# One scattered array for a routed layer's expert outputs, added up in memory, instead of eight arrays added up on VectorE

## The chip, the cores and the metric

The kernel runs on one core of a Trainium2 chip. A core has five engines with a queue of instructions each: TensorE (PE), VectorE (DVE), ScalarE (ACT), GpSimd (POOL) and SyncE (SP). They meet only at semaphores. SP and POOL also issue DMAs, which 16 DMA engines carry out. The metric is the device time of one execution in microseconds (us), as the median of the runs shown. "PEclk" in a view of the profile is the granted TensorE clock as a share of 2.4 GHz.

## The reference

Two layers run one after the other on a batch of 8 x 256 tokens of 128 numbers (float32). Each layer adds an attention-like block and a routed feed-forward block to its input. The change lies in the first layer:

```
xn  = layernorm(x)
x   = x + _L0_attn_ref(xn, ...)          # a selective scan over 256 positions, 16 states, 256 channels
        + _L0_ffn_ref(xn, ...)           # 8 experts
...
# _L0_ffn_ref
scores = softmax(xt @ Wr)                # [2048 tokens, 8 experts]
G, idx = top_k(scores.T, 512)            # every expert takes its 512 best tokens
X_in   = xt[idx]
h      = gelu(einsum('ekd,edh->ekh', X_in, W1) + b1)
X_e    = einsum('ekh,ehd->ekd', h, W2) + b2
out    = zeros.at[idx.reshape(-1)].add(G[..., None] * X_e)
```

Within one expert a token occurs at most once; several experts may take the same token, so their rows for it have to be added.

## The kernel before

The first layer goes through three stages. In the first (up to some 88 us) the tokens are normalized, the scan's inputs are made and the 512 tokens of each expert are found. The second is the **expert stage** (88 to 185 us), the third the **scan**, in 8 batches of 16 steps (185 to 375 us). The second layer follows.

**The expert stage.** For each expert e (0 to 7):

- DVE compares numbers for a one-hot table (`one_hot`, L541), PE turns it into a list of tokens (`compact`, L1216), DVE writes the list (`indices`, L548 and L549).
- POOL issues four indirect DMAs (`gather(e, q)`, L1976), 128 token rows each, from the array `token_rows` in HBM into `xg[e]`. There are four buffers `xg`, so gather e waits for expert e - 4 (`ye_ready`).
- PE turns the rows over (`turn_rows`, L1225), multiplies (`up0`, L1234), ACT applies the gelu (L1755), PE multiplies again (`down0`, L1243; it signals `d_ready`).
- DVE adds the bias and multiplies by the gate (`gated(e)`, L559 and L561) into one of two buffers `ye[e % 2]`, and signals `ye_ready`. From expert 2 on it first waits until the rows that were put from this buffer before have landed (`added0` or `added1`).
- POOL issues four indirect DMAs (`put(e)`, L2013) that write the 512 rows of `ye` to their tokens' places in an array of that expert, `expert_rows{e}`, in HBM. SP has filled the eight arrays with zeros in the first stage (L936, 1 MB each).
- SP reads the whole array back (`rows_in(e)`, 1 MB, L966 and L969) into staging space, and DVE adds it to the sum `acc` in four instructions (`row_sum(e)`, L565). Experts 0 to 5 are added between the `gated` of later experts, the last ones before the scan's first instruction; expert 6 in batch 1 and expert 7 in batch 2, behind steps 3, 5, 7 and 9.

The order in each queue is written out by hand. POOL's is: gathers 0 to 3, put 0, gather 4, put 1, gather 5, and so on to gather 7, put 4, put 5, put 6, a small product (`pro_c`, L1967), put 7, and then the scan. `AHEAD` is 3. DVE's is: `indices(e + 3)`, `gated(e)`, `one_hot(e + 4)`, `row_sum(e - 2)`; ahead of `gated(7)` it makes four bands for the first batch (`band`, L533).

**The scan.** In each step DVE runs two scan instructions on the step's ring slot (L615), POOL multiplies the slot by the C rows (L1988), PE adds it up (`y_pair`, L1185), and ACT fills the slot for the next batch (L1700). PE makes the scan's other input (`fill`, L1175) two steps at a time, behind DVE. Experts' staging space lies in the half of the ring that steps 8 to 15 use, so ACT waits at step 8 of batch 0 until six row sums are done (`row_sum`).

Of the kernel before, what the change touches and what calls it, by code (L numbers as in the profile page):

```python
# [5 lines left out]
F32 = mybir.dt.float32  # L6
# [3 lines left out]
ALU = mybir.AluOpType  # L10
# [62 lines left out]
def layer_pair(nc, x, cf, mask_d, bits_i, bits_f, cols, conv_t, w_up1, w_up2, w_ll, a_log, a_log_t, w_down,  # L73
               wr0, w1_0, w2_0, b2_0, wq, wk, wv, wg, wo, wr1, br1, w1_1, w2_1, b_1, out):
    ctx = ExitStack()
    with ctx:
# [3 lines left out]
        def sem(name):  # L80
# [227 lines left out]
        def own_steps(last):  # L308
            return BY_DVE_LAST if last else BY_DVE
# [23 lines left out]
        def _(dve):  # L333
# [228 lines left out]

            def sum_rows(e, q):

                link.more(V.tensor_tensor(acc[:, 4 * q:4 * q + 4, :].rearrange("p t d -> p (t d)"),  # L565
                                          acc[:, 4 * q:4 * q + 4, :].rearrange("p t d -> p (t d)"),
                                          staged[e][q // 2][:, q % 2 * CH:(q % 2 + 1) * CH], ALU.add))

            def rows_summed():
                dve.wait_ge(S["dve_link"], link.n)  # L570
                dve.sem_inc(S["row_sum"], 1)

            def row_sum(e):

                dve.wait_ge(S[f"rows_in{e % 2}"], 16 * (e // 2 + 1))
                if e == 0:
                    dve.wait_ge(S["bias_in"], 1)
                for q in range(4):
                    sum_rows(e, q)
                rows_summed()  # L580

# [27 lines left out]
            def main(b, par, last=False):  # L609
                for s in range(16):  # L610
# [284 lines left out]
        def _(sp):  # L895
# [58 lines left out]

            def rows_in(e):

                sp.wait_ge(S[f"added{e % 2}"], 64 * (e // 2 + 1))
                if e == E0 - 1:
                    sp.wait_ge(S["row_sum"], E0 - 1)
                elif e == E0 - 2:  # L960
                    sp.wait_ge(S["d_ready"], E0)
                elif e > 1:
                    sp.wait_ge(S["row_sum"], e - 1)
                src = moe[e].rearrange("(p t) d -> p (t d)", p=P)
                if e < E0 - 2:
                    sp.dma_start(arena[:, 4096 + T * (e % 2):4096 + T * (e % 2 + 1)], src).then_inc(S[f"rows_in{e % 2}"], 16)  # L966
                else:
                    for k in range(2):
                        sp.dma_start(staged[e][k], src[:, 8 * P * k:8 * P * (k + 1)]).then_inc(S[f"rows_in{e % 2}"], 16)  # L969

# [4 lines left out]
            for e in range(2, 4):  # L975
# [15 lines left out]
            sp.wait_ge(S["ab_ready"], 7 * 16)  # L991
            for dst, src in ((maskd, mask_d[:, 0:HEADS * SC].rearrange("p (h c) -> p h c", h=HEADS)[:, :, 0:P]),
# [614 lines left out]
        def _(act):  # L1607
# [312 lines left out]
        def _(pool):  # L1920
# [87 lines left out]

            def put(e):

                pool.wait_ge(S["ye_ready"], e + 1)
                for q in range(4):
                    nc.gpsimd.indirect_dma_start(  # L2013
                        out=moe[e], out_offset=bass.IndirectOffsetOnAxis(ap=idx[:, 4 * e + q:4 * e + q + 1], axis=0),
                        in_=ye[:, e % 2, q, :], in_offset=None).then_inc(S[f"added{e % 2}"], 16)
# [12 lines left out]
            for b in range(NB):
# [120 lines left out]
```

## Time and profile before

| | |
|---|---|
| median of 3 runs | 578.55 us (577.93 to 581.52) |
| the profiled execution's own time | 577.68 us |
| its span from the first to the last instruction | 575.8 us |
| mean granted TensorE clock | 0.936 |
| busy, share of the span: PE / DVE / ACT / POOL | 85% / 74% / 53% / 65% |
| chain that ended last, by engine | PE 49%, DVE 32%, issue 6%, DMA 4%, POOL 4%, ACT 3% |

Shares of the whole span mix stages with different limits, so the stages are looked at one by one, by windows of time. A timeline row gives the start, the duration, the engine, the line, the operation and its tiles, how many instructions are merged into the row, and in brackets how long the engine stood idle before it and what released it. POOL's timeline shows every indirect DMA as one row: the row is the time in which POOL issues it, and its data land later.

### The profile page before, as it was taken

Reading aid. Unit: us, or ns where it says so; the run is one execution under the profiler, and the core shown is the slowest. Engines: PE = TensorE matmul, PEld = TensorE weight load, DVE = VectorE, ACT = ScalarE, POOL = GpSimd, SP = SyncE. Lnnn points to the kernel's source line nnn. Section 1 sums busy time; section 2 is a strip of 40 time slices with the busy share of each in tenths; the row PEclk is TensorE's granted clock in tenths of the full one; section 3 lists DMA queues with packets and bytes.
Section 4 is the critical chain, followed back from the end, with each engine's and each line's share of the span. In section 5 each row is a group of like instructions: output and inputs, shape, how many; then the busy total and the mean of one; then the engine's idle time right before and its main releaser. Section 6 shows DMA issues by size and latency. Waiting matters only on the chain.

```text
span 575.8 us, 13831 instructions
## 1 busy us (share of the span) xinstructions
PE 490.0 (85%) x4635; PEld 355.2 (62%) x4636; DVE 426.6 (74%) x1039; ACT 302.7 (53%) x704; POOL 376.9 (65%) x331
## 2 busy tenths in 40 slices
PE   2999942998796989989999998887889899999980
PEld 1643321666655766656666676544666899999980
DVE  6456679356228899999999999977667766666664
ACT  2986771433266566575666775146555444444420
POOL 3198627788776989888998998722467345544550
PEclk9799985998897799999999999998799899999995
DMA  7899621444556322330330324079011212222207
GB/s 216 163 247 348 195 77 36 122 152 152 165 187 252 120 112 76 147 149 4 147 142 8 149 97 128 1 251 338 29 50 50 63 41 57 60 58 53 57 9 219
DMA packets 56482, 70.93 MB, mean 123 GB/s; under 512 B 9327, under 2 KB 43206, under 8 KB 53616
## 3 DMA queue, kind: packets, MB, share of 16 engines
q1 hardware_dynamic: 49696, 57.31, 30.4%
q0 software_dynamic: 5392, 11.76, 7.9%
q10 hardware_dynamic: 1344, 1.18, 0.7%
q8 instruction: 32, 0.52, 0.4%
q14 instruction: 18, 0.15, 0.1%
HBM read 50.03 MB, written 21.25 MB: 124 GB/s over the span
## 4 chain that ended last, share of the span: by engine, by line
PE 49%; DVE 32%; issue 6%; DMA 4%; POOL 4%; ACT 3%; SPq 1%; DVEq 0%; POOLq 0%; ACTq 0%
DVE arena L615 15%; PE banks L1590 8%; PE banks L1577 8%; PE banks L1175 5%; PE banks L1185 4%; PE banks L1310 3%; PE banks L1243 3%; DVE acc L565 2%; POOL bd L1976 2%; PE banks L1332 2%; DVE xnw L541 2%; PE banks L1430 2%; PE banks L1234 2%; PE banks L1110 2%; DVE hbuf L774 1%
## 5 line engine op out<-in xcount | busy, mean ns | idle before, releaser
L1988 POOL TENSOR_TENSOR arena<-arena,bd 128x512 f32<-128x512 f32 x125 | 159.3, 1293 | 20.8 <-DVE arena L615 19.4
L615 DVE TENSOR_TENSOR_SCAN arena<-banks,arena 128x256 f32<-128x256 f32 x256 | 155.8, 669 | 3.2 <-PE banks L1175 1.9
L1700 ACT ACTIVATE arena<-delta,nega 128x256 f32<-128x256 f32 x256 | 108.0, 495 | 57.0 <-PE banks L1185 52.4
L2069 POOL DMA_INDIRECT pair_rows<-w1b,xnT x48 | 49.5, 1032 | 59.2 <-DVE w1b L863 53.1
L1590 PE MATMUL banks<-arena,hbuf 128*128 x384 | 54.9, 286 | 0.7 <-issue 0.3
L1976 POOL DMA_INDIRECT bd<-token_rows,zbuf x32 | 38.1, 1191 | 21.8 <-DVE zbuf L549 12.3
L1577 PE MATMUL banks<-xsT,xm 128*128 128x128 f32 x384 | 51.1, 276 | 0.8 <-DVE acc L837 0.8
L1590 PEld LDWEIGHTS banks<-arena,hbuf 128*128 128x128 f32 x384 | 46.5, 191 | 3.8 <-issue 1.8
L1577 PEld LDWEIGHTS banks<-xsT,xm 128*128 128x128 f32 x384 | 46.6, 192 | 1.2 <-DVE acc L837 1.0
L2013 POOL DMA_INDIRECT expert_rows<-z2p,zbuf x32 | 37.6, 1174 | 13.2 <-issue 8.7
L845 DVE COPY xm<-bd 128x512 f32 x48 | 20.6, 429 | 32.0 <-issue 30.1
L1175 PE MATMUL banks<-xnT,xnw 44*128 44x172 f32 x384 | 38.3, 335 | 6.7 <-DVE arena L615 6.0
L1175 PE MATMUL banks<-hbuf,xnw 44*128 44x172 f32 x384 | 36.7, 323 | 5.7 <-DVE arena L615 5.5
L1175 PEld LDWEIGHTS banks<-xnT,xnw 44*128 44x128 f32 x384 | 29.9, 195 | 15.2 <-issue 8.2
L1755 ACT ACTIVATE hbuf<-banks,colv 128x512 f32<-128x512 f32 x32 | 22.0, 687 | 32.7 <-PE banks L1234 32.0
L2061 POOL DMA_INDIRECT slots_in<-xnw,slot x32 | 31.4, 980 | 11.8 <-issue 8.5
L1905 ACT ACTIVATE xsT<-banks 128x128 f32<-128x128 f32 x48 | 13.2, 278 | 47.8 <-PE banks L1566 47.8
L1175 PEld LDWEIGHTS banks<-hbuf,xnw 44*128 44x128 f32 x384 | 28.4, 186 | 15.0 <-DVE arena L615 7.9
L1913 ACT ACTIVATE hbuf<-banks,b1s 128x128 f32<-128x128 f32 x96 | 30.1, 364 | 11.0 <-PE banks L1577 11.0
L1185 PE MATMUL banks<-arena,z2p 64*64 64x256 f32 x512 | 34.5, 387 | 1.0 <-POOL arena L1988 1.0
L1310 PE MATMUL banks<-z2p,w1b 128*128 128x512 f32 x64 | 33.8, 658 | 1.4 <-ACT xnT L1630 1.4
L1185 PE MATMUL banks<-arena,dga 64*64 64x256 f32 x512 | 34.7, 386 | 0.0
(291 smaller groups left out, 952.4 us busy)
## 6 DMA issues: line engine op xcount, KB each, us to landing
bd<-c_rows SPq DMA_DIRECT2D x16, 1024.0 KB, 5.8
expert_rows<-blank SPq DMA_DIRECT2D x8, 1024.0 KB, 9.0
arena<-expert_rows SPq DMA_DIRECT2D x6, 1024.0 KB, 5.0
bd<-in_w SPq DMA_DIRECT2D x4, 1024.0 KB, 12.5
arena<-in_w SPq DMA_DIRECT2D x4, 1024.0 KB, 13.6
slots_in<-blank POOLq DMA_DIRECT2D x1, 3120.0 KB
xnT<-slots_in SPq DMA_DIRECT2D x48, 65.0 KB, 1.8
xnT<-in_w SPq DMA_DIRECT2D x8, 256.0 KB, 4.5
```

The lines of the kernel that those rows point to most:

```text
L615: m = V.tensor_tensor_scan(ring[:, s, r, :], dw_view(s)[:, 2 * (s % 2) + r, :], ring[:, s, r, :], 0.0, ALU.add, ALU.mult)
L1175: m = pe.matmul(bank[(2 if h == 0 else 0) + j][:, 4 * STARTS[q]:4 * (STARTS[q] + WIN)], xT[rows, par, q, h * P:(h + 1) * P], bands[par][ro ...
L1185: m = pe.matmul(bank[4 + j][64 * h:64 * h + 64, 0:L], weights(h)[rows, :], moving(h)[rows, :], start=start, stop=stop, skip_group_check=True)
L1310: m = pe.matmul(bank[q][:, :], wconv[:, k, h * P:(h + 1) * P], z2p[:, 2 * j:2 * j + 2, k:k + L], start=(k == 0), stop=(k == K - 1))
L1577: m = pe.matmul(bank[2 * (u % 2) + c // 2][:, c % 2 * P:(c % 2 + 1) * P], w1s[:, u % 2, c * P:(c + 1) * P], xsT[:, u % 2, :], start=True, ...
L1590: m = pe.matmul(bank[6 + u % 2][:, 0:P], hT[:, u % 2, c * P:(c + 1) * P], w2r[:, bass.ds(e, 1), c, :], start=(c == 0), stop=(c == HC - 1))
L1700: m = nc.scalar.activation(ring[:, s, r, :], delta[:, half(s), bass.ds(b * L, L)], ACT.Exp, scale=negs[:, half(s), n:n + 1])
L1976: nc.gpsimd.indirect_dma_start(out=xg[e][:, q, :], out_offset=None, in_=rows, in_offset=bass.IndirectOffsetOnAxis(ap=idx[:, 4 * e + q:4 * ...
L1988: nc.gpsimd.tensor_tensor(ring[:, s, :, :], ring[:, s, :, :], c_view(par, s), ALU.mult).then_inc(S["z_pool"], 1)
L2013: nc.gpsimd.indirect_dma_start(out=moe[e], out_offset=bass.IndirectOffsetOnAxis(ap=idx[:, 4 * e + q:4 * e + q + 1], axis=0), in_=ye[:, e % ...
L2061: nc.gpsimd.indirect_dma_start(out=xd, out_offset=bass.IndirectOffsetOnAxis(ap=slot[:, w, t:t + 1], axis=0), in_=xnw[:, t, :], in_offset=N ...
L2069: nc.gpsimd.indirect_dma_start(out=yd, out_offset=bass.IndirectOffsetOnAxis(ap=xs[:, u, P:P + 1].bitcast(I32), axis=0), in_=ys[:, u % 4, : ...
```

## The change

There is one array `expert_rows` instead of eight, zeroed by one DMA. The puts add into it (`compute_op=ALU.add`). A put begins only when the put of the expert before has landed, since two experts may add to one row. SP reads the array back once, between the C rows of batch 3 and of batch 4, and DVE adds it to `acc` in batch 4 behind steps 3, 5, 7 and 9. The row sums of the expert stage and of batches 1 and 2 go, with their semaphore. On POOL each gather stands ahead of the put that it used to follow, and the four puts of expert 7 stand in batches 1 and 2, ahead of the products of steps 4 and 11.

```diff
-        moe = [nc.dram_tensor(f"expert_rows{e}", [T, P], F32, kind="Internal").ap() for e in range(E0)]
+        moe = nc.dram_tensor("expert_rows", [T, P], F32, kind="Internal").ap()
...
-                if e > 1:
-                    row_sum(e - 2)
...
-                    if b in (1, 2) and 2 < s < 11 and s % 2:
-                        e = E0 - 3 + b
+                    if b == 4 and 2 < s < 11 and s % 2:
                         if s == 3:
-                            dve.wait_ge(S[f"rows_in{e % 2}"], 80)
-                            dve.wait_ge(S["dn_evac"], 1 + b)
-                        sum_rows(e, (s - 3) // 2)
+                            dve.wait_ge(S["rows_in"], 32)
+                            dve.wait_ge(S["dn_evac"], 5)
+                        sum_rows((s - 3) // 2)
                         if s == 9:
-                            rows_summed()
+                            dve.wait_ge(S["dve_link"], link.n)
...
-            for e in range(E0):
-                sp.dma_start(moe[e].rearrange("(p k) d -> p k d", p=P), blank[:, None, 0:P].broadcast_to([P, NT, P])
-                             ).then_inc(S["moe_zero"], 16)
+            sp.dma_start(moe.rearrange("(p k) d -> p k d", p=P), blank[:, None, 0:P].broadcast_to([P, NT, P])
+                         ).then_inc(S["moe_zero"], 16)
...
+            def rows_in():
+                sp.wait_ge(S["d_ready"], E0)
+                for w in range(2):
+                    sp.wait_ge(S[f"added{w}"], 64 * (E0 // 2))
+                for k in range(2):
+                    sp.dma_start(staged[k], moe.rearrange("(p t) d -> p (t d)", p=P)[:, 8 * P * k:8 * P * (k + 1)]
+                                 ).then_inc(S["rows_in"], 16)
...
-            for e in range(4):
-                weights(e + 4)
-                rows_in(e)
-            rows_in(4)
-            rows_in(5)
-            c_spread(0)
-            rows_in(6)
-            c_spread(1)
-            rows_in(7)
-            for b in range(2, NB):
+            for e in range(4, E0):
+                weights(e)
+            for b in range(NB):
                 c_spread(b)
+                if b == 3:
+                    rows_in()
...
-                    if b == 0 and s == 8:
-                        act.wait_ge(S["row_sum"], E0 - 2)
...
+            def put(e, q):
+                if q == 0:
+                    pool.wait_ge(S["ye_ready"], e + 1)
+                    if e:
+                        pool.wait_ge(S[f"added{(e - 1) % 2}"], 64 * ((e - 1) // 2 + 1))
+                    else:
+                        pool.wait_ge(S["moe_zero"], 16)
+                nc.gpsimd.indirect_dma_start(
+                    out=moe, out_offset=bass.IndirectOffsetOnAxis(ap=idx[:, 4 * e + q:4 * e + q + 1], axis=0),
+                    in_=ye[:, e % 2, q, :], in_offset=None, compute_op=ALU.add).then_inc(S[f"added{e % 2}"], 16)
...
                 for s in range(16):
+                    if b in (1, 2) and s in (4, 11):
+                        put(E0 - 1, b * 2 - 2 + s // 8)
...
             for e in range(E0):
                 for q in range(4):
                     gather(e, q)
-                if e == AHEAD:
-                    pool.wait_ge(S["moe_zero"], 8 * 16)
-                if e >= AHEAD:
-                    put(e - AHEAD)
-            for e in range(E0 - AHEAD, E0):
-                if e == E0 - 1:
+                if e > AHEAD:
+                    for q in range(4):
+                        put(e - AHEAD - 1, q)
+            for e in range(E0 - AHEAD - 1, E0 - 1):
+                if e == E0 - 2:
                     pro_c(0)
-                put(e)
+                for q in range(4):
+                    put(e, q)
```

POOL's queue in the expert stage before, from the last gather that has no put behind it (`bd` holds the gathered rows, `z2p` the buffers `ye`):

```order
L1976 DMA bd<-token_rows,zbuf 128x136 x3
L2013 DMA expert_rows0<-z2p,zbuf 2048x128 [waits ye_ready,moe_zero]
L2013 DMA expert_rows0<-z2p,zbuf 2048x128 x3
L1976 DMA bd<-token_rows,zbuf 128x136 [waits ye_ready,id_ready,rows_g]
L1976 DMA bd<-token_rows,zbuf 128x136 x3
L2013 DMA expert_rows1<-z2p,zbuf 2048x128 [waits ye_ready]
```

The same place now, and, behind the left-out rows, the queue's end before the scan:

```order
L1944 DMA bd<-token_rows,zbuf 128x136 x3
L1944 DMA bd<-token_rows,zbuf 128x136 [waits ye_ready,id_ready,rows_g]
L1944 DMA bd<-token_rows,zbuf 128x136 x3
L1957 DMA expert_rows<-z2p,zbuf 2048x128 [waits moe_zero,ye_ready]
L1957 DMA expert_rows<-z2p,zbuf 2048x128 x3
...
L1957 DMA expert_rows<-z2p,zbuf 2048x128 [waits added0,ye_ready]
L1957 DMA expert_rows<-z2p,zbuf 2048x128 x3
L1935 TENSOR_TENSOR cb<-ccur,bcur 16x256 [waits pro_xe]
L1957 DMA expert_rows<-z2p,zbuf 2048x128 [waits added1,ye_ready]
L1957 DMA expert_rows<-z2p,zbuf 2048x128 x3
L1970 TENSOR_TENSOR arena<-arena,bd 128x512 [waits scanned,c_in00]
```

Gather 4 has moved ahead of put 0, every put but the first has a second wait (`added`), and the scan's first product stands behind put 6 instead of put 7.

DVE's queue before, from the gate of expert 6 to the scan's first instruction (`xnT<-step_pat` are the bands):

```order
L559 TENSOR_TENSOR z2p<-banks,zbuf 128x512 [waits dve_link,added0,d_ready]
L561 TENSOR_TENSOR z2p<-z2p,bd 128x512 [waits dve_link]
L565 TENSOR_TENSOR acc<-acc,arena 128x512 [waits rows_in0]
L565 TENSOR_TENSOR acc<-acc,arena 128x512 x3
L533 TENSOR_TENSOR xnT<-step_pat,banks 128x516 [waits dve_link,pro_bt]
L533 TENSOR_TENSOR xnT<-step_pat,banks 128x516 [waits pro_bt] x3
L559 TENSOR_TENSOR z2p<-banks,zbuf 128x512 [waits added1,d_ready]
L561 TENSOR_TENSOR z2p<-z2p,bd 128x512 [waits dve_link]
L565 TENSOR_TENSOR acc<-acc,arena 128x512 [waits rows_in1]
L565 TENSOR_TENSOR acc<-acc,arena 128x512 x3
L615 SCALAR_TENSOR_TENSOR arena<-banks,arena 128x256 [waits dve_link,dw_ready,ab_ready]
```

The same place now:

```order
L558 TENSOR_TENSOR z2p<-banks,zbuf 128x512 [waits added0,d_ready]
L560 TENSOR_TENSOR z2p<-z2p,bd 128x512 [waits dve_link]
L532 TENSOR_TENSOR xnT<-step_pat,banks 128x516 [waits pro_bt] x4
L558 TENSOR_TENSOR z2p<-banks,zbuf 128x512 [waits added1,d_ready]
L560 TENSOR_TENSOR z2p<-z2p,bd 128x512 [waits dve_link]
L598 SCALAR_TENSOR_TENSOR arena<-banks,arena 128x256 [waits dw_ready,ab_ready]
```

The row sums are gone, and the scan's first instruction now follows the gate of expert 7, which still waits (`added1`) until put 5 has landed.

## Rows read from the trace of the kernel before

**Rows 1.** Windows: expert stage, then batches 1, 2 and 3 (busy time, instructions).
```profile
core 0: us, PE busy (x) PEld busy (x) DVE busy (x) ACT busy (x) POOL busy (x), PEclk, DMA share, GB/s
111.70:161.10 49.40, 43.03 (x285) 31.67 (x284) 23.62 (x34) 16.70 (x26) 39.67 (x32) 0.93 0.49 164
208.90:234.20 25.30, 22.66 (x288) 15.60 (x286) 25.09 (x44) 15.62 (x37) 22.27 (x18) 1.00 0.26 90
234.20:259.80 25.60, 22.63 (x288) 15.57 (x286) 25.39 (x45) 15.74 (x37) 22.29 (x18) 1.00 0.30 121
259.80:282.50 22.70, 22.28 (x288) 15.29 (x285) 22.64 (x40) 15.07 (x37) 20.51 (x18) 1.00 0.25 95
```

**Rows 2.** Timeline, POOL: a fill of the first stage, expert stage, start of the scan.
```profile
13.59 2.38 POOL L1934 DMA_DIRECT2D slots_in<-blank  x1
...
111.97 1.95 POOL L2013 DMA_INDIRECT expert_rows<-z2p,zbuf  x1 [0.30 <-issue]
...
119.35 2.88 POOL L1976 DMA_INDIRECT bd<-token_rows,zbuf  x1 [0.30 <-DVE z2p L561]
...
127.62 2.95 POOL L2013 DMA_INDIRECT expert_rows<-z2p,zbuf  x1 [0.30 <-DVE z2p L561]
...
143.55 0.97 POOL L2013 DMA_INDIRECT expert_rows<-z2p,zbuf  x1 [0.30 <-issue]
...
159.69 1.41 POOL L1976 DMA_INDIRECT bd<-token_rows,zbuf  x1 [0.30 <-issue]
...
175.52 1.17 POOL L2013 DMA_INDIRECT expert_rows<-z2p,zbuf  x1 [3.88 <-DVE z2p L561]
...
187.89 9.85 POOL L1988 TENSOR_TENSOR arena<-arena,bd 128x512 f32<-128x512 f32 x8
```

**Rows 3.** Timeline, SP's DMA queue: the read-back of expert 2.
```profile
145.84 0.33 SPq L966 DMA_DIRECT2D arena<-expert_rows  x1
```

**Rows 4.** Timeline, DVE, expert stage and the scan's first instructions.
```profile
119.10 2.28 DVE L541 TENSOR_TENSOR xnw<-cfs,zbuf 128x2048 bf16<-128x2048 f32 x1
...
134.44 0.69 DVE L559 TENSOR_TENSOR z2p<-banks,zbuf 128x512 f32<-128x512 f32 x1 [1.79 <-PE banks L1243]
...
135.78 2.28 DVE L541 TENSOR_TENSOR xnw<-cfs,zbuf 128x2048 bf16<-128x2048 f32 x1
...
181.54 2.93 DVE L565 TENSOR_TENSOR acc<-acc,arena 128x512 f32<-128x512 f32 x4
184.69 3.60 DVE L615 TENSOR_TENSOR_SCAN arena<-banks,arena 128x256 f32<-128x256 f32 x6 [0.21 <-DVE acc L565]
```

**Rows 5.** Timeline, PE, expert stage.
```profile
122.33 3.74 PE L1243 MATMUL banks<-w2b,hbuf 128*128 128x128 f32 x32
125.90 3.60 PE L1234 MATMUL banks<-bd,w1b 128*128 128x512 f32 x8
...
130.67 3.74 PE L1243 MATMUL banks<-w2b,hbuf 128*128 128x128 f32 x32
...
140.81 1.12 PE L1225 MATMUL banks<-ident,bd 128*128 128x128 f32 x4 [2.14 <-DMA bd<-token_rows,zbuf]
...
152.97 0.66 PE L1225 MATMUL banks<-ident,bd 128*128 128x128 f32 x4 [3.12 <-DMA bd<-token_rows,zbuf]
```

**Rows 6.** POOL's DMAs by line: durations (ns, minimum/median/maximum), landing of puts, then of gathers.
```profile
L2013 POOL DMA_INDIRECT expert_rows<-z2p,zbuf x32: 966/976/2947, 112.0 to 186.9; - x32
DMA to landing us min/median/max: 2.3/2.4/6.4
...
DMA to landing us min/median/max: 2.5/3.2/6.0
...
L2069 POOL DMA_INDIRECT pair_rows<-w1b,xnT x48: 982/1054/1143, 463.8 to 559.7; - x48
```

**Rows 7.** Timeline, batch 3: POOL's products of steps 9 to 13, PE's sum behind step 10.
```profile
273.99 6.19 POOL L1988 TENSOR_TENSOR arena<-arena,bd 128x512 f32<-128x512 f32 x5
...
280.58 1.09 PE L1185 MATMUL banks<-arena,z2p 64*64 64x256 f32 x16
```

More of the change, by code:

```diff
@@ L191, in layer_pair @@
                xnT[:, HID * (e % 4 + 2):HID * (e % 4 + 3)].rearrange("p (c d) -> p c d", c=HC) for e in range(E0)]
-        staged = [[arena[:, 4096 + T * (e % 2) + 8 * P * k:4096 + T * (e % 2) + 8 * P * (k + 1)] if e < E0 - 2 else (w1f, w2f)[k]
-                   for k in range(2)] for e in range(E0)]
+        staged = (w1f, w2f)
         rows = nc.dram_tensor("token_rows", [T, ROW], F32, kind="Internal").ap()
         crows = nc.dram_tensor("c_rows", [2, N * L], F32, kind="Internal").ap()
-        moe = [nc.dram_tensor(f"expert_rows{e}", [T, P], F32, kind="Internal").ap() for e in range(E0)]
+        moe = nc.dram_tensor("expert_rows", [T, P], F32, kind="Internal").ap()
         latef = delta[:, :, :].rearrange("p h t -> p (h t)")
@@ L264, in layer_pair @@
                  "u_ready h_ready d_ready w_in0 w_in1 w_in2 w_in3 b2_in rows_x gates_ready rows_g moe_zero hot_ready cp_ready id_ready "
-                 "xg_in0 xg_in1 xg_in2 xg_in3 xg_in4 xg_in5 xg_in6 xg_in7 xg_ps xg_sb ye_ready added0 added1 rows_in0 rows_in1 row_sum "
+                 "xg_in0 xg_in1 xg_in2 xg_in3 xg_in4 xg_in5 xg_in6 xg_in7 xg_ps xg_sb ye_ready added0 added1 rows_in "
                  "abs_r exp_r sm_exp ln_r cnt_in cnt_out "
@@ L561, in gated, with sum_rows @@
                 V.tensor_tensor(y, y, xg[e][:, :, P + e:P + e + 1].broadcast_to([P, 4, P]), ALU.mult).then_inc(S["ye_ready"], 1)
-            def sum_rows(e, q):
+            def sum_rows(q):
                 link.more(V.tensor_tensor(acc[:, 4 * q:4 * q + 4, :].rearrange("p t d -> p (t d)"),
                                           acc[:, 4 * q:4 * q + 4, :].rearrange("p t d -> p (t d)"),
[L567 to L579, printed above, removed]
-                rows_summed()
+                                          staged[q // 2][:, q % 2 * CH:(q % 2 + 1) * CH], ALU.add))
             one_hot(0)
@@ L621, in main @@
                         mult(b, par, s - 1, last)
-                    if b in (1, 2) and 2 < s < 11 and s % 2:
-                        e = E0 - 3 + b
+                    if b == 4 and 2 < s < 11 and s % 2:
                         if s == 3:
-                            dve.wait_ge(S[f"rows_in{e % 2}"], 80)
-                            dve.wait_ge(S["dn_evac"], 1 + b)
-                        sum_rows(e, (s - 3) // 2)
+                            dve.wait_ge(S["rows_in"], 32)
+                            dve.wait_ge(S["dn_evac"], 5)
+                        sum_rows((s - 3) // 2)
                         if s == 9:
-                            rows_summed()
+                            dve.wait_ge(S["dve_link"], link.n)
                     if s == 2:
@@ L953, in c_spread @@
                                  ).then_inc(S[f"c_in{par}{k}"], 16)
-            def rows_in(e):
-                sp.wait_ge(S[f"added{e % 2}"], 64 * (e // 2 + 1))
-                if e == E0 - 1:
[L959 to L969, printed above, removed]
+            def rows_in():
[5 more added lines that the diff above has]
+                                 ).then_inc(S["rows_in"], 16)
             for e in range(2):
@@ L2007, in _ @@
                 less_rest(c)
[L2009 to L2015, printed above, removed]
             for e in range(E0):
@@ L2019, in _ @@
                     gather(e, q)
-                if e == AHEAD:
-                    pool.wait_ge(S["moe_zero"], 8 * 16)
-                if e >= AHEAD:
-                    put(e - AHEAD)
-            for e in range(E0 - AHEAD, E0):
-                if e == E0 - 1:
+                if e > AHEAD:
[3 more added lines that the diff above has]
+                if e == E0 - 2:
                     pro_c(0)
-                put(e)
+                for q in range(4):
+                    put(e, q)
             for b in range(NB):
```

## The prediction

> **What bounds the kernel now.** I read the page's chain of waits first: PE and DVE hold 81% of it, POOL 4%. That is a mean over stages, so I went to windows and timelines. In batch 3 PE is busy for 22.28 of 22.70 us and DVE for 22.64 [rows 1]; batches 1 and 2, which hold four row sums each, last 25.3 and 25.6 with DVE as full, PE at 22.6 and POOL at 22.3. So a batch with sums is DVE's, and costs 2.6 to 2.9 more. The expert stage is different: from 111.7 to 161.1 POOL works through 32 indirect DMAs that are busy for 39.67 of 49.4, and the rest is the 0.30 gap ahead of each [rows 1, 2]. PE needs 8.34 per expert while nothing holds it (122.33 to 130.67), and later it waits 2.14 and 3.12 for gathered rows [rows 5]: POOL issues, and PE follows. POOL's last put stands directly ahead of the scan's first product, at 187.89 [rows 2]; DVE's first scan comes at 184.69, behind a row sum of 2.93 [rows 4]. The views to use are therefore POOL's timeline for the expert stage and DVE's for the batches.
>
> Two prices from POOL's timeline carry the sum. An undisturbed put takes 0.97, and with the gap a DMA costs 1.27. The last put of expert 2 starts at 143.55 and the read-back that waits for it is issued at 145.84 [rows 2, 3], so a plain put has landed 2.3 after its start; all puts land in 2.3 to 6.4 by their own view, median 2.4 [rows 6].
>
> **Part 1, the expert stage.** Two unknowns: d, by which an adding put occupies POOL longer than a plain one, and x, by which it lands later.
>
> *Up to put 3.* Before, put 0 to gather 7 (eight groups of four) run from 111.97 to 161.10 [rows 2]. Now the same eight groups run as gather 4, put 0, ... gather 7, put 3; gather 4 can start at 111.97, since expert 0 is through. The 32 DMAs were busy for 39.67, undisturbed they would be 32 x 0.97 = 31.0, so 8.6 are stalls. Beside the one-hots, DMAs of 1.95, 2.88 and 2.95 appear [rows 2, 4], 1.0, 1.9 and 2.0 too long; a fourth one-hot (135.78) I give 1.9. These 6.8 stay. The other 1.8 lie beside the row sums and go. Put 3 then ends at 161.1 - 1.8 = 159.3, plus 16 d.
>
> *Puts 4 and 5.* Each now starts when the one before has landed. Put 3 starts at 159.3 - 4 x 1.27 = 154.2 and lands 3 x 1.27 + 2.3 = 6.1 later, at 160.3 + 16 d + x. Puts 4 and 5 each take 6.2 + 4 d + x from landing to landing (0.1 for the semaphore): put 5 lands at 172.7 + 24 d + 3 x.
>
> *Who is late next.* Gate 7 waits for that landing, since it writes the same buffer; it takes two instructions, 1.35, and nothing stands behind it but the scan: first scan at 174.2 + 24 d + 3 x, against 184.69 [rows 4]. The other path is PE's. Put 1 now goes a group later, at 132.0 + 4 d, and lands at 138.1 + 8 d + x, so gate 3 starts there instead of at 134.44 [rows 4]; expert 7 is through PE four periods later, at 138.1 + 4 x 8.34 = 171.5 + 8 d + x, plus a little for the first batch's preparation. At d = x = 0 that is about even with put 5, with any d or x put 5 is later. Put 6 keeps POOL for 5.1 + 4 d more, so the first product lags the first scan's end by 2 to 3, as it does now.
>
> *The prices.* The trace holds no adding put. For d: zero is the floor, since adding takes nothing off a put; a scatter with one more option, the bounds check, takes 1.054 against 0.976 [rows 6], which is 0.08; the longest DMA that POOL issues anywhere takes 2.38 [rows 2], which gives d = 1.4. I take 0.1, by the nearest row, the scatter. For x: zero is the floor; a put and a gather laid end to end (2.3 + 2.5) give x = 2.5. I take 0.8, what a gather, which reads rows of HBM, lands later than a put at the median (3.2 against 2.4) [rows 6]. Then 24 d + 3 x = 4.8, the scan starts at 179.0, and the stage is **5.7 shorter**.
>
> The Trainium skill ("DMA: Bandwidth & Descriptors", section "Latency and other measured facts") puts an access to HBM at 0.2 us on average and 2 us under high load. An estimate from that page alone would set x to 0.2 or 2 and the end 1.8 lower or 3.6 higher than by the gather's row; no run here shows an adding put, so the trace can't choose yet. The same page (section "Rules for kernel authors") says that an accumulating DMA reads its destination and writes it later, so that any other write in between is lost, and wants a wait for the earlier DMA's semaphore: the three waits are its price.
>
> **Part 2, the batches.** Batches 1 and 2 lose their sums and become like batch 3; batch 4 gets four sums: 25.3 + 25.6 + 22.7 become 22.6 + 22.7 + 25.5, **2.8 shorter**. The moved puts add 2 x (1.27 + d) = 2.7 to POOL in each of batches 1 and 2, which has 20.51 in 22.7 [rows 1]: 23.2, a lag of 2.7 at most, of which some 0.5 is carried on. What covers it: POOL ends step 10's product at 273.99 + 2 x 1.24 = 276.5 and PE takes it up at 280.58 [rows 7], 4.1 later, the smallest such distance that I found in the batch. The put's own waits there are over long before. Cost nothing; without the cover, the lag beyond 4.1.
>
> **Edits costed at nothing.** Seven zero fills and seven read-backs (14 MB) go: no step of PE or DVE ahead of 88 us waits for them, and SP's weights for the experts come earlier than they are used. ACT's wait at step 8 goes; it was over when the scan began. The one read-back waits for the last put, in step 11 of batch 2, and is used a whole batch later.
>
> **The sum.** 577.68 - 5.7 - 2.8 = 569.2 in terms of the profiled execution. The median of the runs stands 0.87 above that: **570**.
>
> **Rivals.**
>
> *1. An adding put keeps POOL much longer (slower).* Everything from put 0 to put 5 stands in one queue, so d counts 24 times. With d = x = 0 the end would be 577.68 - 10.5 - 2.8 + 0.87 = 565.3, and 24 d + 3 x comes on top. It is over 1% slower (above 584.3) from 24 d + 3 x = 19, at x = 0.8 from d = 0.69: a put of 1.67. At d = 0.9 it ends at 589, at d = 1.4 at some 605, with batches 1 and 2 then past the 4.1 too. For it: POOL has no slack in this stage, and no row of this trace prices a DMA that adds. Against it: gathers, scatters and the scatter with a check all take 0.97 to 1.05, and even the fill of 3 MB only 2.38. Chance 0.2.
>
> *2. The waits take back what the shorter queue gives (within 1%).* x between 1.7 and 2.5 with d of 0.1 to 0.3, or d of 0.2 to 0.6: 573 to 583. At x = 2.2 and d = 0.15 it is 565.3 + 6.6 + 3.6 = 575.5. For it: the waits are in series, and landings up to 6.4 occur. Against: nothing else uses the DMA engines much once the read-backs are gone. Chance 0.24.
>
> *3. The puts in batches 1 and 2 stretch them.* With the 2.95 that a put took beside a one-hot, two cost 6.5 per batch, 2.4 past the cover in batch 1 and some 4 in batch 2: 576. Against it: the instructions that such DMAs stood beside, one-hots and row sums, are in neither batch. Chance 0.04.
>
> **Chances and range.** The forecast (565 to 573) has 0.52, which is also the chance of faster by over 1% (below 572.8), about what a measurement of this kernel can tell from no change. Rivals 2 and 3 make 0.28 for within 1%; rival 1 makes 0.20 for slower. The range begins at the floor of both prices, 565, and reaches to 584, through rivals 2 and 3 and to the point where rival 1 decides.
>
> **What the changed profile would show.** Right: four adding puts in a row 1.3 to 1.5 apart on POOL; POOL idle for 2 to 2.5 ahead of puts 4, 5 and 6, released by a DMA; gate 7 released by a put's landing, the first scan near 179; batches 1 and 2 at 22.7 with no idle DVE, batch 4 at 25.5. Wrong: adding puts of 1.6 or more; a first scan later than 185; PE idle ahead of its sums in batches 1 and 2, waiting for POOL; or PE's path ending after put 5's landing, which would make gate 7 wait for PE.

## The result, and the profile after

The changed kernel takes 588.96 us (median, 584.73 to 589.83) beside 580.02 for the kernel before in the same comparison: ratio 1.0142, 95% interval 1.0079 to 1.0206. The forecast was 570 with a range from 565 to 584, so the time lies 5 above the range. The profiled execution took 589.83, with a span of 588.0 against 575.8.

All of the loss lies ahead of the scan. The first scan starts at 198.57 instead of 184.69 [rows 4], 13.9 us later; the batches give 2.4 back, and 0.7 is lost behind them: 12.2, the difference of the spans. Windows of the changed kernel (columns as in [rows 1]: the same stretch of the expert stage, then batches 0 to 4):

```profile
111.70:161.10 49.40, 39.55 (x250) 29.15 (x248) 15.70 (x21) 15.74 (x25) 38.33 (x28) 0.86 0.39 81
198.57:223.06 24.49, 20.47 (x218) 14.71 (x220) 22.04 (x39) 11.19 (x27) 23.58 (x20) 0.78 0.34 98
223.06:245.83 22.77, 22.35 (x288) 15.37 (x286) 22.52 (x40) 15.11 (x37) 22.45 (x20) 1.00 0.32 100
245.83:268.60 22.77, 22.35 (x288) 15.38 (x286) 22.65 (x40) 15.51 (x39) 22.44 (x20) 1.00 0.32 103
268.60:291.38 22.78, 22.36 (x288) 15.38 (x286) 22.66 (x41) 15.53 (x39) 21.95 (x20) 1.00 0.38 138
291.38:316.80 25.42, 22.56 (x288) 15.58 (x286) 25.39 (x44) 16.14 (x38) 22.29 (x18) 1.00 0.23 85
```

Batches 1 and 2 are as long as batch 3, and batch 4 carries the sums, as predicted. In the expert stage POOL still works all the time, but for one wait of 3.15 (shown below), and it issues 28 instructions instead of 32. The price of one is in its view of the tile (durations in ns, minimum/median/maximum; to be laid beside [rows 6]):

```profile
L1957 POOL DMA_INDIRECT expert_rows<-z2p,zbuf x32: 1550/1565/2586, 121.2 to 263.7; - x32
...
  DMA expert_rows<-z2p,zbuf: 13.4, 3
...
DMA to landing us min/median/max: 3.2/3.3/11.5
```

An adding put keeps POOL for 1.565 instead of 0.976: d = 0.59. The middle row is what POOL waited for ahead of puts 4, 5 and 6, 13.4 us in three waits. POOL's timeline (start, duration; the wait before it in brackets):

```profile
111.32 1.21 POOL L1944 DMA_INDIRECT bd<-token_rows,zbuf  x1 [0.30 <-issue]
115.68 0.94 POOL L1944 DMA_INDIRECT bd<-token_rows,zbuf  x1 [3.15 <-DVE zbuf L548]
...
121.17 2.59 POOL L1957 DMA_INDIRECT expert_rows<-z2p,zbuf  x1 [0.30 <-issue]
...
168.51 1.56 POOL L1957 DMA_INDIRECT expert_rows<-z2p,zbuf  x1 [0.30 <-issue]
172.49 1.55 POOL L1957 DMA_INDIRECT expert_rows<-z2p,zbuf  x1 [2.42 <-DMA expert_rows<-z2p,zbuf]
...
178.06 1.56 POOL L1957 DMA_INDIRECT expert_rows<-z2p,zbuf  x1 [0.30 <-issue]
188.27 1.57 POOL L1957 DMA_INDIRECT expert_rows<-z2p,zbuf  x1 [8.64 <-DMA expert_rows<-z2p,zbuf]
...
204.48 11.63 POOL L1970 TENSOR_TENSOR arena<-arena,bd 128x512 f32<-128x512 f32 x9
```

Two rows were not foreseen. At 115.68 gather 4 has waited 3.15 for its indices, in a place where put 0 ran before [rows 2]. At 188.27 put 5 has waited 8.64 for put 4, where the put ahead of it waited 2.42 for the same kind of landing. On SP's DMA queue one transfer starts beside it, the C rows of batch 0 for all partitions, 2 MB in two DMAs:

```profile
177.40 0.33 SPq L927 DMA_DIRECT2D c_rows<-ccur  x1
178.85 0.81 SPq L934 DMA_DIRECT2D bd<-c_rows  x2
```

(The first row puts these C rows into HBM, from where the second spreads them.)

DVE's timeline shows what these landings hold: gates 2 to 7 all wait for a put (2, 5, 6 and 7 are shown), and the scan follows gate 7.

```profile
131.29 0.69 DVE L558 TENSOR_TENSOR z2p<-banks,zbuf 128x512 f32<-128x512 f32 x1 [8.01 <-DMA expert_rows<-z2p,zbuf]
...
171.85 0.69 DVE L558 TENSOR_TENSOR z2p<-banks,zbuf 128x512 f32<-128x512 f32 x1 [11.39 <-DMA expert_rows<-z2p,zbuf]
...
187.57 0.69 DVE L558 TENSOR_TENSOR z2p<-banks,zbuf 128x512 f32<-128x512 f32 x1 [14.30 <-DMA expert_rows<-z2p,zbuf]
...
197.24 0.69 DVE L558 TENSOR_TENSOR z2p<-banks,zbuf 128x512 f32<-128x512 f32 x1 [5.84 <-DMA expert_rows<-z2p,zbuf]
...
198.57 3.59 DVE L598 TENSOR_TENSOR_SCAN arena<-banks,arena 128x256 f32<-128x256 f32 x6
```

Put 4's last DMA was issued at 178.06, and gate 6 could start at 187.57: 9.5 later, where gate 5 started 3.3 behind put 3's last (168.51 to 171.85). The theory to be tested, **A**: 24 x 0.59 = 14.2 us, the price of adding on POOL, is most of the loss; **C**: the broadcast held up put 4's landing, some 6 us; **G**: gather 4's wait is worth 3. The main rival, **B** or **W**: it is not the price of the instruction but the new order, and the waits from one landing to the next.

### The profile page after: what moved, and what is told of

Same layout as the page of the kernel before. It is cut to its first block, busy times and chain, and to the rows that moved or that the text cites. A ratio compares the mean times of both kernels' runs of the same rounds, so it can differ in the third digit from the quotient of the medians.

```text
span 588.0 us, 13779 instructions
## 1 busy us (share of the span) xinstructions
PE 493.5 (84%) x4635; PEld 359.7 (61%) x4636; DVE 408.8 (70%) x1011; ACT 302.0 (51%) x704; POOL 384.2 (65%) x331
## 4 chain that ended last, share of the span: by engine, by line
PE 50%; DVE 26%; DMA 7%; POOL 7%; issue 6%; ACT 3%; DVEq 1%; SPq 1%; POOLq 0%; ACTq 0%
DVE arena L598 10%; PE banks L1560 7%; PE banks L1145 7%; PE banks L1547 7%; PE banks L1155 6%; POOL expert_rows L1957 5%; DMA expert_rows<-z2p,zbuf 4%; PE banks L1280 3%; DVE xnw L540 2%; PE banks L1302 2%; PE banks L1080 2%; PE banks L1400 2%; DVE hbuf L756 1%; POOL bd L1944 1%; DMA z2p<-pair_rows 1%
## 5 line engine op out<-in xcount | busy, mean ns | idle before, releaser
L1957 POOL DMA_INDIRECT expert_rows<-z2p,zbuf x32 | 52.3, 1633 | 21.7 <-DMA expert_rows<-z2p,zbuf 13.4
L1944 POOL DMA_INDIRECT bd<-token_rows,zbuf x32 | 36.1, 1129 | 24.6 <-DVE zbuf L548 15.5
L558 DVE TENSOR_TENSOR z2p<-banks,zbuf 128x512 f32<-128x512 f32 x8 | 5.5, 691 | 65.5 <-DMA expert_rows<-z2p,zbuf 58.0
L1145 PE MATMUL banks<-xnT,xnw 44*128 44x172 f32 x384 | 40.1, 347 | 10.9 <-DVE xnT L532 6.1
L1145 PEld LDWEIGHTS banks<-xnT,xnw 44*128 44x128 f32 x384 | 31.5, 204 | 19.3 <-DVE xnT L532 7.4
L1723 ACT ACTIVATE hbuf<-banks,colv 128x512 f32<-128x512 f32 x32 | 22.0, 687 | 34.4 <-PE banks L1204 33.7
```

The source lines that it names most:

```text
L1145: m = pe.matmul(bank[(2 if h == 0 else 0) + j][:, 4 * STARTS[q]:4 * (STARTS[q] + WIN)], xT[rows, par, q, h * P:(h + 1) * P], bands[par][ro ...
L1944: nc.gpsimd.indirect_dma_start(out=xg[e][:, q, :], out_offset=None, in_=rows, in_offset=bass.IndirectOffsetOnAxis(ap=idx[:, 4 * e + q:4 * ...
L1957: nc.gpsimd.indirect_dma_start(out=moe, out_offset=bass.IndirectOffsetOnAxis(ap=idx[:, 4 * e + q:4 * e + q + 1], axis=0), in_=ye[:, e % 2, ...
```

## The experiments

Medians in us; each ratio is against the kernel before, run on the same chip, where its median lay between 578.9 and 581.6; small differences between medians of two comparisons carry this spread. First scan and batch 0 are read from DVE's timeline of the profiled execution (32 scans make a batch).

| run | median | ratio, 95% interval | first scan | batch 0 |
|---|---|---|---|---|
| changed kernel | 588.96 | 1.0142 (1.0079 to 1.0206) | 198.6 | 24.5 |
| 1 plain puts | 572.90 | 0.9889 (0.9848 to 0.9931) | 181.0 | 24.5 |
| 2 broadcast held | 584.57 | 1.0070 (1.0039 to 1.0101) | 194.7 | 25.2 |
| 3 both | 567.21 | 0.9779 (0.9747 to 0.9811) | 179.7 | 22.2 |
| 4 before, adding | 590.85 | 1.0181 (1.0133 to 1.0228) | 195.4 | 24.7 |
| 5 order as before | 586.98 | 1.0120 (1.0038 to 1.0201) | 194.4 | 25.4 |
| 6 put 7 and C, B late | 600.75 | 1.0404 (1.0317 to 1.0491) | 193.6 | 35.3 |
| 7 two arrays, held | 579.03 | 0.9990 (0.9953 to 1.0028) | 188.7 | 24.6 |
| 8 mixed | 571.17 | 0.9860 (0.9784 to 0.9935) | 179.9 | 25.5 |
| 9 mixed pairs | 575.59 | 0.9921 (0.9893 to 0.9949) | 176.7 | 25.4 |
| 10 mixed, late sum | 571.05 | 0.9860 (0.9803 to 0.9918) | 176.5 | 25.4 |
| 11 put 7 alone | 596.78 | 1.0326 (1.0265 to 1.0387) | 194.4 | 33.7 |

**1. The changed kernel with plain puts.**

```diff
-  in_=ye[:, e % 2, q, :], in_offset=None, compute_op=ALU.add)
+  in_=ye[:, e % 2, q, :], in_offset=None)
```

> The changed kernel with puts that overwrite instead of add (the sums of the rows are left out); order, waits and the one array stay. In the changed kernel's trace an adding put holds POOL for 1.56 us, against 0.98 for a plain one. Theory A (the price on POOL): 24 puts stand ahead of the scan's first instruction, so 24 x 0.59 = 14 us go, and some 1 us of later landings: about 574 us against the changed kernel's 589. Theory B (the waits for a landing cost the time, whatever the put costs): three to four waits of 2.4 us stay, and the price lies beside them: about 585. Theory C (put 4's landing is held up by the broadcast of the C rows, 9.4 us instead of 3.3) says nothing against either; its 6 us stay here if a landing that is waited for still meets the broadcast.

572.90, 16.1 below the changed kernel with every wait still in place; B falls. The put's view of its tile in this run, and put 5 on POOL's timeline:

```profile
L1957 POOL DMA_INDIRECT expert_rows<-z2p,zbuf x32: 963/972/1953, 120.6 to 245.9; - x32
...
168.89 0.96 POOL L1957 DMA_INDIRECT expert_rows<-z2p,zbuf  x1 [2.06 <-DMA expert_rows<-z2p,zbuf]
```

**2. The broadcast held back.** SP now sends batch 0's C rows only when put 5 has landed.

```diff
 def c_spread(b):
     par = b % 2
+    if b == 0:
+        sp.wait_ge(S["added1"], 64 * 3)
```

> The changed kernel, with the broadcast of the C rows for batch 0 held back until put 5 has landed. Theory C: put 4 lands 3.3 us after its last issue instead of 9.4, gate 6, put 5 and gate 7 come 6 us earlier, and the time is about 583 us against 589. If put 4's late landing has another cause, the landing stays at 9 us and the time at 589, or gets longer, since POOL's first product waits for the broadcast.

584.57, 4.4 less. POOL's timeline, the start of put 4's last DMA and of put 5:

```profile
179.21 1.56 POOL L1959 DMA_INDIRECT expert_rows<-z2p,zbuf  x1 [0.30 <-issue]
184.37 1.57 POOL L1959 DMA_INDIRECT expert_rows<-z2p,zbuf  x1 [3.59 <-DMA expert_rows<-z2p,zbuf]
```

The wait of 8.64 is 3.59, so C holds in the main; that it is not 2.42 stays open. The scan starts 3.8 earlier, and 0.8 of that goes again in batch 0. The intervals of this run and of the changed kernel overlap a little, so the wait is the firmer evidence, and runs 6 and 11 add to it below.

**3. Both edits together.**

> Both edits together: plain puts (the sums of the rows are left out) and the broadcast held back until put 5 has landed. Theories A and C together: 574 - 6 = 568 us, close to the 570 that the blind sum gave with its cheap put. If only A holds: 574. If only C holds: 580.

567.21, and DVE's gate 7 now waits for PE, no longer for a landing:

```profile
178.33 0.69 DVE L558 TENSOR_TENSOR z2p<-banks,zbuf 128x512 f32<-128x512 f32 x1 [0.40 <-PE banks L1215]
```

The first scan, 179.7, is 0.7 from the 179.0 of the prediction, but by chance: the 179.0 held 4.8 for an adding put, and for plain puts (d = x = 0) the formula gives 174.2. The scan comes 5.5 later than that. Gather 4's wait, 3.15 in the changed kernel, is in this run too, and the path that ends last is now PE's, which the prediction had at 171.5 "plus a little" and which ends at 178.3. Against run 2 the scan starts 15.1 earlier, and batch 0 is 3.1 shorter.

**4. The kernel before, adding.** Its 32 puts add into their own zeroed arrays; nothing else is changed.

```diff
-  in_=ye[:, e % 2, q, :], in_offset=None)
+  in_=ye[:, e % 2, q, :], in_offset=None, compute_op=ALU.add)
```

> The kernel before with one edit: its puts add into their eight zeroed arrays (same result). Nothing waits for a landing that did not wait before. Theory A: the 32 puts take 0.59 us more each on POOL, 19 us, of which the 3.9 us that POOL stood idle ahead of put 6 may cover some: about 593 to 597 us against 579. Theory B: the price alone costs little, 579 to 582.

590.85: the option alone, with no array, order or wait changed, costs 10.9, a little less than A expected. Its tile:

```profile
L2013 POOL DMA_INDIRECT expert_rows<-z2p,zbuf x32: 1552/1564/2890, 113.4 to 198.8; - x32
```

The rest of the change, everything but the adding, is thus worth some 2 us at most while puts add (588.96 against 590.85); the intervals of the two overlap, so it may be nothing.

**5. The order of before, in the changed kernel.**

```diff
-    if e > AHEAD:
+    if e >= AHEAD:
         for q in range(4):
-            put(e - AHEAD - 1, q)
-for e in range(E0 - AHEAD - 1, E0 - 1):
+            put(e - AHEAD, q)
+for e in range(E0 - AHEAD, E0 - 1):
```

> The changed kernel, with adds, waits, the one array and the late put 7 kept, but each put directly behind a gather as in the kernel before (gathers 0 to 3, put 0, gather 4, put 1, gather 5, ...). Theory G (gathers ahead of puts costs here, because gather 4 waits 3.15 us for its indices while put 0 could already go): the 3.15 us go, and gathers 4 to 7 now cover the landings of puts 0 to 3, so first scan at 192 to 196 instead of 198.6 and 583 to 586 us. Rival H (the order is what saves the kernel from worse: gathers 6 and 7 then come two puts of 7.5 us later and PE waits for them): 590 to 595 us. Between, 587 to 589: the order is worth nothing either way.

586.98, just above G's range: the scan starts 4.1 earlier, as G has it, batch 0 takes 0.9 longer, and the interval covers no difference from the changed kernel. POOL's timeline shows put 0 in the gap, and the broadcast now holding up put 5, which put 6 waits for:

```profile
113.00 3.18 POOL L1957 DMA_INDIRECT expert_rows<-z2p,zbuf  x1 [0.30 <-issue]
...
178.90 1.57 POOL L1957 DMA_INDIRECT expert_rows<-z2p,zbuf  x1 [2.62 <-DMA expert_rows<-z2p,zbuf]
...
193.75 1.56 POOL L1957 DMA_INDIRECT expert_rows<-z2p,zbuf  x1 [7.61 <-DMA expert_rows<-z2p,zbuf]
```

**6 and 11. Put 7 ahead of the scan again.** In run 6 POOL's small product for the C and B columns (`pro_c`) went behind put 6 with it; run 11 leaves that in its place.

```diff
-  if b in (1, 2) and s in (4, 11):
-      put(E0 - 1, b * 2 - 2 + s // 8)
-for e in range(E0 - AHEAD - 1, E0 - 1):
+for e in range(E0 - AHEAD - 1, E0):
     if e == E0 - 2:          # run 6: E0 - 1
         pro_c(0)
```

> The changed kernel with put 7 back ahead of the scan instead of in batches 1 and 2. It must wait 2.4 us for put 6's landing and takes 4 x 1.87 us, so POOL's first product starts some 10 us later than in the changed kernel, while DVE's first scan stays at 198.6. Theory M (moving put 7 is worth POOL's lag, since DVE's ring runs full in batch 0): 593 to 599 us. Rival N (POOL is fast enough to make up the lag in batches 1 and 2, which then have no puts): 588 to 590 us.

> The changed kernel with put 7 ahead of the scan, as in the run before of this kind, but with POOL's first small product for the C and B columns kept ahead of put 6, where the changed kernel has it. In that run it stood behind put 6 as well, at 199.45, TensorE waited 13.6 us for it, and batch 0 took 35.2 us; so the run did not price the move of put 7 alone. Theory M (POOL's products start 2.4 + 7.5 us later, the ring fills, TensorE idles at its lower clock): batch 0 still 30 us or longer, 595 to 600 us on the footing where the changed kernel has 589. Rival V (nearly all of the delay was the small product): batch 0 at 25 to 28 us, 589 to 592 us.

596.78 for the move alone, 7.8 above the changed kernel, though the scan starts 4.2 earlier in the profiled execution; M holds, V falls. Run 6 has a median 4 higher, above M's range for it, but its times spread from 593 to 605 and the intervals of the two overlap; N falls. DVE's timeline of run 11, and then POOL's:

```profile
206.45 2.43 DVE L598 TENSOR_TENSOR_SCAN arena<-banks,arena 128x256 f32<-128x256 f32 x4 [0.89 <-PE banks L1145]
218.55 3.82 DVE L598 TENSOR_TENSOR_SCAN arena<-banks,arena 128x256 f32<-128x256 f32 x6 [9.66 <-PE banks L1145]
```
```profile
203.41 1.55 POOL L1957 DMA_INDIRECT expert_rows<-z2p,zbuf  x1 [2.52 <-DMA expert_rows<-z2p,zbuf]
...
210.00 11.61 POOL L1968 TENSOR_TENSOR arena<-arena,bd 128x512 f32<-128x512 f32 x9
```

With POOL's first product at 210.0 instead of 204.48, PE waits 7.51 for it and DVE stands still for 9.66 in the middle of batch 0. So the late put 7 is a part of the change that pays, 7.8 us.

Up to put 5 both runs are the changed kernel, and still their scans start earlier, by 4.2 in run 11 and 5.0 in run 6. POOL's timeline of run 11, put 4's last DMA and put 5, and then of run 6:

```profile
176.56 1.56 POOL L1957 DMA_INDIRECT expert_rows<-z2p,zbuf  x1 [0.30 <-issue]
184.00 1.57 POOL L1957 DMA_INDIRECT expert_rows<-z2p,zbuf  x1 [5.88 <-DMA expert_rows<-z2p,zbuf]
```
```profile
178.46 1.56 POOL L1957 DMA_INDIRECT expert_rows<-z2p,zbuf  x1 [0.30 <-issue]
183.17 1.57 POOL L1957 DMA_INDIRECT expert_rows<-z2p,zbuf  x1 [3.15 <-DMA expert_rows<-z2p,zbuf]
```

The broadcast was issued at 177.86 and 180.12, so 1.3 and 1.7 behind put 4's last instead of 0.8, and put 5 waited 5.88 and 3.15 instead of 8.64. That speaks for C. It also says that the changed kernel's first scan, 198.6, is one execution's: a scan that starts some 4 earlier, as in runs 2 and 5, does not by itself show what an edit is worth.

**7. Two arrays.** Even and odd experts add into an array each, so a put waits for the one two before it, which its gate has awaited already. The broadcast is held as in run 2.

```diff
-  if e:
-      pool.wait_ge(S[f"added{(e - 1) % 2}"], 64 * ((e - 1) // 2 + 1))
+  if e > 1:
+      pool.wait_ge(S[f"added{e % 2}"], 64 * (e // 2))
...
-  out=moe, ...
+  out=moe[e % 2], ...
```

> The changed kernel with the broadcast of batch 0 held until put 5 has landed (584.6 us by itself), and even and odd experts adding into two arrays, so that a put waits for the put two before it and not for the one just before. Only the even array is read back: the odd experts' rows are left out of the sum. Theory A (nearly all of the loss is the 1.56 us that an adding put keeps POOL, 24 x 0.59 = 14 us): the three waits of 2 to 3.6 us ahead of puts 4, 5, 6 go, but gates 6 and 7 still wait for puts 4 and 5: first scan 3 to 5 us earlier, 579 to 582 us, still above the 568 to 573 us of plain puts. Rival W (the serial order of the adds is the loss): 570 to 575 us.

579.03, as A has it: POOL's waits for the put before are gone, and 5.5 us with them. So of the 17.4 between runs 2 and 3, which differ in the adding alone, most stays where no put waits for the one before; W falls. The Trainium skill ("DMA: Bandwidth & Descriptors", section "Rules for kernel authors") asks for that wait before anything else writes the destination; run 7 against run 2 shows its price here, 5.5 us.

**8. Mixed: a kernel with the same result.** Experts 0 to 5 put plain into six arrays, 0 to 4 are summed in the expert stage, and puts 6 and 7 add into the sixth; put 0 goes ahead of gather 4, and the broadcast is held.

```diff
+for what, e in (("p", 0), ("g", 4), ("p", 1), ("g", 5), ("g", 6), ("p", 2),
+                ("g", 7), ("p", 3), ("p", 4), ("p", 5), ("c", 0), ("p", 6)):
+    ...
+to = moe[min(e, E0 - 3)]     # compute_op=ALU.add for e > E0 - 3 alone
```

> A kernel with the same result from the pieces: experts 0 to 5 put plain into six arrays of their own; 0 to 4 are read back and added in the expert stage, where DVE is idle for over half of the time; puts 6 and 7 add into the sixth array (8 adding scatters instead of 32, put 7's in batches 1 and 2), which is read back and added in batch 4. Order on POOL: gathers 0 to 3, put 0, gather 4, put 1, gathers 5 and 6, put 2, gather 7, puts 3 to 6. The broadcast of batch 0 is held until put 5 has landed. By theory A with the landing beside the broadcast and the early put 0: POOL has 44 x 1.27 us from 112 to 168 with few waits, gate 7 between 170 and 178, first scan at 172 to 180: 560 to 568 us. Rival R (read-backs of 1 MB beside the puts' landings hold these up, as the broadcast did): 570 to 576 us.

571.17, 1.4% below the kernel before and 17.8 us below the changed one, but 3 to 11 above what was expected. That is R's range, but not by R's mechanism: put 6 starts 4.1 behind put 5's last DMA (171.49 to 175.57), and 4.0 in run 3, which has no read-backs there (174.16 to 178.13). DVE's timeline shows what stands ahead of the scan:

```profile
173.49 2.50 DVE L565 TENSOR_TENSOR acc<-acc,arena 128x512 f32<-128x512 f32 x4 [0.90 <-DMA arena<-expert_rows]
176.13 2.50 DVE L533 TENSOR_TENSOR xnT<-step_pat,banks 128x516 f32<-128x516 f32 x4
...
179.88 3.59 DVE L615 TENSOR_TENSOR_SCAN arena<-banks,arena 128x256 f32<-128x256 f32 x6
```

Expert 4's sum stands ahead of the bands, and PE, which waits for these, idles for 1.52. Windows of this run ahead of the scan and in it, for PE and its granted clock:

```profile
174.90:177.40 2.50, 0.98 (x11) 0.79 (x11) 2.35 (x5) 2.50 (x7) 1.82 (x1) 1.00 0.22 39
...
182.40:184.90 2.50, 2.45 (x16) 2.11 (x18) 2.50 (x5) 0.00 (x0) 2.50 (x3) 0.50 1.13 220
```

Behind the gap the clock is at its lower level, 1.2 GHz (0.50), and batch 0 takes 25.5. In run 3 the mean clock of batch 0 was 0.92 and it took 22.2:

```profile
179.70:201.80 22.10, 19.73 (x230) 14.02 (x228) 21.86 (x38) 16.71 (x41) 21.47 (x19) 0.92 0.46 182
```

**9 and 10. Mixed pairs.** Put 6 adds into expert 4's array and put 7 into expert 5's; expert 4's array is summed in batch 2 (run 9) or 3 (run 10). The diff is against run 8.

```diff
-to = moe[min(e, E0 - 3)]
+to = moe[e if e < E0 - 2 else e - 2]
...
-if b == 4 and 2 < s < 11 and s % 2:
+if b in (2, 4) and 2 < s < 11 and s % 2:      # run 10: (3, 4)
```

> As the mixed kernel (six arrays, experts 0 to 5 put plain, the broadcast of batch 0 held, put 7 in batches 1 and 2), but put 6 adds into expert 4's array and put 7 into expert 5's, so that neither waits for a landing that is still on its way (the 2.46 us ahead of put 6 go), and array 4 is read back and added in batch 2 instead of at 173.5 in the expert stage. Theory P (in the mixed kernel the row sum at 173.49 held the first bands back, TensorE idled ahead of the scan, its granted clock fell to 0.50 for 12 us and batch 0 took 25.4 us instead of the 22.1 that it took with plain puts): first scan at 176 to 178 instead of 179.9, batch 0 at 22 to 23 us, batch 2 2.7 us longer: 565 to 568 us. Rival Q (the gap ahead of the scan is there anyway, and the second sum in the batches takes back what the first scan gains): 570 to 573 us.

> As the mixed pairs, with one thing moved: array 4 is added in batch 3, which has none of put 7's scatters, instead of in batch 2, which has two. In the mixed pairs batch 2 took 31.7 us: two of the four adds of a quarter array took 2.2 us there instead of 0.7, one beside a put on POOL, DVE's scans then waited for PE, and the granted clock of the batch was 0.78. Theory S (a row sum and a put in one batch collide): batch 2 at 22.8 us, batch 3 at 25.5, so 6 us less than the mixed pairs on the same footing: 568 to 571 us. Rival T (the sum is slow wherever it stands, for another reason): batch 3 at 30 us or more, 574 to 577 us.

In both the scan starts some 3 earlier, as P has it, but batch 0 stays at 25.4, so that half of P fell. Windows of run 9 ahead of the scan and in it:

```profile
175.00:177.50 2.50, 2.50 (x29) 2.16 (x28) 2.15 (x4) 2.50 (x8) 1.92 (x2) 1.00 0.69 116
...
180.00:182.50 2.50, 2.50 (x22) 2.13 (x21) 2.50 (x6) 2.20 (x6) 2.50 (x3) 0.50 1.03 361
```

The gap ahead of the scan is gone: PE is busy up to it and behind its start idles for 0.94, as long as in run 3. Yet the clock is at 0.50 for 10.2 us from 179.2 on, and in run 3 for 3.4 alone. So batch 0 goes with the time that the clock is low, and PE's gap does not by itself decide that; what does stays open. At 575.59 run 9 misses the ranges of both P and Q: it loses the rest in batch 2, 31.7 long. DVE's timeline there, three of the sum's four quarters, and then POOL's:

```profile
230.41 2.16 DVE L565 TENSOR_TENSOR acc<-acc,w1b 128x512 f32<-128x512 f32 x1
...
234.84 2.26 DVE L565 TENSOR_TENSOR acc<-acc,w1b 128x512 f32<-128x512 f32 x1
...
239.97 0.66 DVE L565 TENSOR_TENSOR acc<-acc,w2b 128x512 f32<-128x512 f32 x1
```
```profile
220.37 11.64 POOL L1999 TENSOR_TENSOR arena<-arena,bd 128x512 f32<-128x512 f32 x9
...
233.84 2.70 POOL L1999 TENSOR_TENSOR arena<-arena,bd 128x512 f32<-128x512 f32 x2
```

In run 10 batch 2 is at 22.8 again and batch 3 at 27.6, not the 25.5 of S nor the 30 of T; one quarter still took 2.67 there, with no put in the batch. The rows show when a quarter is slow: all three slow ones began while POOL ran its products without a gap, and ended 0.56 behind the last of these (232.57 and 232.01, 237.10 and 236.54; in run 10 255.72 and 255.16). The quick ones began in a gap of POOL's or in its first product behind one. So POOL's products seem to hold the add up, not a put; and POOL may have had no gap there because the moved puts had made it late. Both are read from rows, and no run tests them. Moving the sum out of the puts' batch is worth about 4 us. Run 10 ends level with run 8, at the upper end of S's range.

## Why the prediction was wrong

- **The step that failed is the price d of the adding put.** It was taken as 0.1, from a scatter with a bounds check, and is 0.59; it counts 24 times, so 14.2 instead of 2.4. Neither the scatter nor any other plain DMA stood for it; only the two bounds, 0 and 1.4, held. Rival 1 named this mechanism; but its point for 1% slower, 0.69, was not reached.
- **x** was taken as 0.8 and is 0.36: a put that adds holds up the next one for 2.42, a plain one for 2.06 (run 1). The Trainium skill ("DMA: Bandwidth & Descriptors", section "Latency and other measured facts") puts an access to HBM at 0.2 us on average and 2 us under load; the measured 0.36 is nearer its lower figure.
- With both measured prices its own formula gives 565.3 + 14.2 + 1.1 = 580.6, within 1% of before and inside its range. Two waits that it did not have, at nothing in its sum, add the rest.
- **Put 4's landing beside the broadcast**: put 5 waits 8.64 instead of 2.42, 6.2 us. That "nothing else uses the DMA engines much once the read-backs are gone" was wrong. The read-backs had also kept the broadcast back on SP's queue: before, it left 8.0 us after ACT had the rows ready at 171.83, now 1.5 after (177.38 to 178.85). And put 4, at 161.40 before, starts 11 later and now meets it. Run 2 shows 4.4 us of it by the medians, 3.8 at the first scan. SP's queue before:

```profile
174.00 0.42 SPq L945 DMA_DIRECT2D c_rows<-ccur  x1
179.83 0.82 SPq L952 DMA_DIRECT2D bd<-c_rows  x2
```

- **"Gather 4 can start at 111.97"** was wrong: its indices come from DVE only at 114.9, and it starts at 115.68, 3.15 late. Run 5, which puts put 0 there, starts the scan 4.1 earlier, but its time does not tell the gain apart from none. With these two the sum is 580.6 + 6.2 + 3.1 = 589.9, against 588.96. So close a fit is partly luck: runs 2 and 5 give back 4.4 and 2.0 by their medians, less than the 6.2 and 3.1 in the sum.
- Right were the path (gates 5 to 7 and put 5's landing, not PE, set the first scan), POOL's waits ahead of puts 4 and 6, and **the batches**: 25.3, 25.6 and 22.7 [rows 1], with 22.8 for batch 4, became 22.8, 22.8, 22.8 and 25.4, 2.6 less against the 2.8 predicted. Rival 3 did not come about: the moved puts took 1.59, and DVE was busy for 22.5 of 22.8 or more in batches 1 and 2.
- Not in the sum at all was the clock: batch 0 takes 22.2 where the clock was at 0.50 for 3.4 us of it (run 3), and 24.2 to 25.5 where it was for 10 to 13 (before, the changed kernel, and runs 1, 2, 4, 5 and 7 to 10). Here it hardly counted, 24.2 before and 24.5 after.

## What to carry to other kernels

Count how often an unknown price stands in the queue that bounds a stage before you take the nearest row for it: at 24 times, half a microsecond decides. When transfers are removed, ask what they had kept back, on their own queue too, and what it now lands beside. Use an accumulating scatter only where it replaces work on the path, and not for all eight experts: runs 8 and 10 add for the last two alone and take 571. These runs also hold the broadcast and move put 7, and no run takes the part of the adding from the rest.

## What the runs showed of the hardware

- A scatter of 128 rows that adds takes POOL 1.56 us, a plain one 0.97, into one array or into eight (the changed kernel and run 4; the kernel before and run 1).
- A small scatter that was issued 0.8 ahead of a broadcast of 2 MB on another queue held up DVE until 9.5 after its issue, another one until 3.3. POOL's wait for it was 8.64, 5.88 and 3.15 with the broadcast issued 0.8, 1.3 and 1.7 behind it (the changed kernel, runs 11 and 6), and 3.59 with the broadcast held (run 2).
- An add of two SBUF operands on DVE (128x512) took 0.66 in a gap of POOL's products and 2.16 to 2.67 where these followed each other without one; it then ended 0.56 behind the last (runs 9 and 10).
- With idle times of PE of 0.94 to 1.81 around the scan's start its granted clock was at 0.50 while it worked again, for 3.4 us in run 3, 10.2 in run 9 and 13.7 in run 8; batch 0 lasted 22.2, 25.4 and 25.5.
